# Windowed attention by key block, split low-rank products, and an earlier split of the third FFN tile

## What is computed

```python
def lora_proj(h, Wb, A, Bm, scale):
    return h @ Wb.T + h @ A.T @ Bm.T * scale
...
Q, K, V = (lora_proj(h, w, A, B, 1/16) for each of q, k, v)   # 16 heads of 128, rank 16
valid = (j <= i) & (j >= i - 63)                              # window of 64 keys
attn = softmax(rope(Q) @ rope(K).T / sqrt(128) + mask)
out  = lora_proj(attn @ V, wo, oA, oB, 1/16)
...
y = sum over experts e of cw[:, e] * (silu(x @ wg[e].T) * (x @ wu[e].T)) @ wd[e].T   # + a shared expert
```

## Time and profile before

| | |
|---|---|
| median of 3 runs | 1549.61 us (1549.12 to 1550.35) |
| the profiled execution | 1545.96 us, span 1544.1 us |
| PE busy | 1426.9 us, 92% of the span |
| VectorE (DVE), ScalarE (ACT), GpSimd (POOL) busy | 1112.4, 856.4, 627.5 us |
| first attention | up to about 338 us |
| output projection, first FFN, second attention | to 396, to about 630, to about 1265 us |
| second projection and second FFN | the rest |

### The profile page before, as it was taken

The page is one execution under the profiler, slowest core; times in us unless marked ns, Lnnn a source line. Parts: engine busy times, 40 slices in busy tenths (PEclk is TensorE's granted clock), DMA queues, the critical chain, the costliest instruction groups (busy, mean ns, idle before and its releaser), DMA issues.

```text
span 1544.1 us, 27763 instructions
## 1 busy us (share of the span) xinstructions
PE 1426.9 (92%) x8632; PEld 1197.3 (78%) x8632; DVE 1112.4 (72%) x2132; ACT 856.4 (55%) x1917; POOL 627.5 (41%) x540
## 2 busy tenths in 40 slices
PE   6999999999899999788988889789898989899998
PEld 4888888888788888667776777667777769688887
DVE  5666666657565556579999998899999977565555
ACT  1444444454343333477777777677777765433332
POOL 3555555530000001376868686668686620000000
PEclk8999999999999999999999999999999999999999
DMA  3000000001111112110101010101010001111110
GB/s 110 25 25 26 25 24 24 16 23 44 49 42 51 41 51 73 38 28 21 35 18 39 15 39 17 33 20 37 17 28 18 18 21 43 49 52 51 41 51 28
DMA packets 30138, 54.25 MB, mean 35 GB/s; under 512 B 6273, under 2 KB 13761, under 8 KB 29761
## 3 DMA queue, kind: packets, MB, share of 16 engines
q1 hardware_dynamic: 30016, 52.78, 11.7%
HBM read 39.13 MB, written 1.05 MB: 26 GB/s over the span
## 4 chain that ended last, share of the span: by engine, by line
PE 69%; DVE 14%; issue 9%; ACT 4%; POOL 1%; DVEq 0%; ACTq 0%; POOLq 0%
PE ps L1187 49%; PE ps L1388 8%; PE ps L1495 6%; PE ps L1333 5%; DVE pt_lo L706 3%; DVE nmb L691 2%; DVE qh L683 2%; PE ps L1275 2%; DVE qh L681 2%; ACT pt_hi L1106 1%; DVE rb L408 1%; ACT pb_low L1096 1%; DVE ot L714 1%; DVE h_lo L600 1%; DVE hf L594 1%
## 5 line engine op out<-in xcount | busy, mean ns | idle before, releaser
L706 DVE TENSOR_TENSOR pt_lo<-ps,pt_hi 128x512 fp32r<-128x512 f32 (+3 forms) x384 | 206.5, 549 | 36.3 <-ACT pt_hi L1106 34.0
L1187 PE MATMUL ps<-kh,qh 128*128 128x512 f32 (+3 forms) x768 | 194.5, 362 | 19.9 <-DVE qh L683 10.8
L1106 ACT CAST pt_hi<-ps 128x512 fp32r<-128x512 f32 (+3 forms) x384 | 176.0, 480 | 60.0 <-PE ps L1495 53.7
L691 DVE TENSOR_REDUCE nmb<-ps 128x1 f32<-128x1024 f32 (+7 forms) x256 | 191.0, 746 | 14.7 <-PE ps L1187 13.3
L1187 PEld LDWEIGHTS ps<-kh,qh 128*128 128x128 f32 x768 | 135.7, 192 | 48.8 <-ACT pb_low L1096 10.3
L1187 PE MATMUL ps<-xt_hi,wf_hi 128*128 128x512 f32 x400 | 160.7, 402 | 9.4 <-DVE wf_lo L522 9.4
L1187 PE MATMUL ps<-pt_hi,vst 128*128 128x512 f32 (+3 forms) x384 | 163.5, 426 | 0.0
L1187 PE MATMUL ps<-xt_hi,wf_lo 128*128 128x512 f32 x400 | 159.3, 398 | 0.0
L1187 PE MATMUL ps<-xt_lo,wf_hi 128*128 128x512 f32 x400 | 159.3, 398 | 0.0
L1032 ACT CAST h_hi<-hf 128x512 fp32r<-128x512 f32 x100 | 62.1, 621 | 137.8 <-DVE hf L594 137.8
L588 DVE TENSOR_TENSOR sg<-sg,cwu 128x512 f32<-128x512 f32 x88 | 62.2, 707 | 105.2 <-ACT sg L1026 105.1
(11 more groups left out here) (169 smaller groups left out, 4082.7 us busy)
## 6 DMA issues: line engine op xcount, KB each, us to landing
wf<-in_wf SPq DMA_DIRECT2D x50, 384.0 KB, 3.0
rb<-raw SPq DMA_DIRECT2D x192, 64.0 KB, 2.0
wa<-in_wa SPq DMA_DIRECT2D x16, 384.0 KB, 3.0
wb<-in_wb SPq DMA_DIRECT2D x8, 384.0 KB, 3.0
wo<-in_wo_a SPq DMA_DIRECT2D x16, 128.0 KB, 2.0
wo<-in_wo_b SPq DMA_DIRECT2D x16, 128.0 KB, 2.0
lb<-in_lb SPq DMA_DIRECT2D x16, 72.0 KB, 3.0
x_res<-in_x SPq DMA_DIRECT2D x4, 256.0 KB, 3.6
```

What stands on the lines that cost most here:

```text
L691: v.tensor_reduce(nmb[:, par, i:i + 1], ps[:, b:b + 2, :].rearrange("p b k -> p (b k)")[:, 0:P * (t + 1)], AX.X, ALU.max, negate=True).the ...
L706: v.tensor_tensor(pt_lo[:, s % 3, at], ps[:, 4 + s % 2, at], pt_hi[:, s % 3, at].bitcast(F32), ALU.subtract).then_inc(sem("b_pt_lo"), 1)
L1106: s_.copy(pt_hi[:, s % 3, at], ps[:, 4 + s % 2, at]).then_inc(sem("b_pt_hi"), 1)
L1187: return t_.matmul(o, l, r, start=start, stop=stop)
```

## The change

- **Values and products.** `xt_hi`, `xt_lo` lose their padding; values are made for eight tiles of 128 keys that are aligned with the query tiles, in four pieces. A key tile is seen by its own query tile and by the first 64 queries of the next, 192 queries, so `products` goes over key tiles: one fp32 matmul of 192 columns each, cut in two where it crosses a PSUM bank. `turn` transposes two squares of 128 and up to two blocks of 64 by 128, `pt` copies 320 or 384 columns instead of 512, and `pta` holds a whole head for each of two heads. The pieces of `products` hold one, two, two and three key tiles, and the third and fourth have new due times.
- **Low-rank products.** `la` and `lb` are loaded twice over (rows 0 to 47 and 64 to 111 of 128). ScalarE casts `lb` to `lb_hi` (`low_rank_hi`), VectorE makes `lb_lo` of 64 rows (`low_rank_lo`), and `lora` is four fp32r matmuls of one pass. `wef` has one buffer instead of two, so `weff(h)` waits for the split of head h-1. The output's `oa` (all heads, one load at the start) and `ob` are split ahead of head 14's steps, 80 rows each, and `low_rank_a` is one fp32r matmul.
- **Third FFN tile.** Its cast and its low part move into the end of the output projection, for both FFNs; the SP program is not changed there.

```diff
-            pta = sb("pta", [P, 2, HALF], c=own)
+            pta = sb("pta", [P, 2, NT * KW], c=own)
...
+            def low_rank_lo(h, u):
+
+                dve.wait_ge(sem("a_lb_hi"), h + 1)
+                v.tensor_tensor(lb_lo[0:LO, u, :], lb[0:LO, u, :], lb_hi[0:LO, u, :].bitcast(F32),
+                                ALU.subtract).then_inc(sem("a_lb_lo"), 1)
+
             def weff(h, u):
...
-                after(dve, "a_w_hi", h - 1)
-                after(dve, "a_w_lo", h - 1)
+                after(dve, "a_w_hi", h)
+                after(dve, "a_w_lo", h)
...
             def head_a(i, ip, u):
-                for kind, dh, n in steps_a(("weff", "rope", "max", "inv"), i, u):
+                if isinstance(i, int) and 2 * i + u == HA - 2:
+
+                    dve.wait_ge(sem("a_oa_hi"), 1)
+                    v.tensor_tensor(oa_s[LO:OR, :, :], oa[LO:OR, :, :], oa_s[LO:OR, :, :].bitcast(F32),
+                                    ALU.subtract).then_inc(sem("a_oa_lo"), 1)
+                    v.tensor_tensor(ob_s[32:LO, :], ob[32:LO, :], ob_s[32:LO, :].bitcast(F32),
+                                    ALU.subtract).then_inc(sem("a_oa_lo"), 1)
+                for kind, dh, n in steps_a(("lb_lo", "weff", "rope", "max", "inv"), i, u):
...
-                    elif h == 14:
+                    elif h == 13:
                         ffn_weight_lo(nxt, 1, 1, 1)
+                    elif h == 15:
+                        ffn_weight_lo(nxt, 2, 2, 0)
...
-                w_lo(2, 2, 0)
...
+            def low_rank_hi(h, u):
+                act.wait_ge(sem(f"lb_loaded{u}"), loads(h, u, 16))
+                after(act, "a_lora", h - 1)
+                s_.copy(lb_hi[:, u, :], lb[:, u, :]).then_inc(sem("a_lb_hi"), 1)
...
+                if isinstance(i, int) and 2 * i + u == HA - 2:
+
+                    act.wait_ge(sem("oa_loaded"), 16)
+                    act.wait_ge(sem("a_ob_loaded"), 16)
+                    act.wait_ge(sem("a_lora"), HA)
+                    s_.copy(ob_s[:, :], ob[:, :])
+                    s_.copy(oa_s[:, :, :], oa).then_inc(sem("a_oa_hi"), 1)
...
                     elif h == 12:
                         ffn_weight_hi(nxt, 1, 1, 1)
+                    elif h == 14:
+                        ffn_weight_hi(nxt, 2, 2, 0)
...
-                ffn_weight_hi(s, 2, 2, 0)
...
                 for c in range(NC):
-                    last = mm(ps[:, c, 0:3 * P], la[:, c, :], lb[:, u, :])
+                    mm(ps[:, c, 0:3 * P], las[:, c, :], lb_hi[:, u, :], True, False)
+                    last = mm(ps[:, c, 0:3 * P], las[0:LO, c, :], lb_lo[0:LO, u, :], False, True)
...
             def products_a(h, i, ip, u, n):
                 pe.wait_ge(sem("a_pt"), 4 * h + n + 1)
-                pe.wait_ge(sem("a_vout"), 5 * i + n + 2)
-                for m in range(2):
-                    t = 2 * n + m
-                    o = ps[:, 2 + 2 * u + t // 4, P * (t % 4):P * (t % 4) + P]
-                    for b in range(2):
-                        last = mm(o, va[:, ip, t + b, u, :], pta[:, n % 2, P * (2 * m + b):P * (2 * m + b) + P],
-                                  b == 0, b == 1)
+                pe.wait_ge(sem("a_vout"), 4 * i + n + 1)
+                for b in range(max(0, 2 * n - 1), 2 * n + 1 if n < 3 else NT):
+                    q, end = P * b, min(P * b + KW, T)
+                    while q < end:
+                        w = min(end, HALF * (q // HALF) + HALF) - q
+                        last = t_.matmul(ps[:, 2 + 2 * u + q // HALF, q % HALF:q % HALF + w], va[:, ip, b, u, :],
+                                         pta[:, u, KW * b + q - P * b:KW * b + q - P * b + w],
+                                         start=b == 0 or q == HALF > P * b, stop=True, skip_group_check=True)
+                        q += w
...
-    "products": [3717, 5961, 10934, 11408],
+    "products": [3717, 5961, 8000, 10934],
...
-    "o_out": [6909, 10401],
+    "o_out": [8300, 10401],
...
+    "lb_hi": [-29900],
+    "lb_lo": [-29800],
```

More of the change, by code:

```diff
@@ L27 @@
 PAD = WIN
[L28 to L29 removed]
 KW = WIN + P
 RANK = 16
+LR = 3 * RANK
+LO = 64
+OR = 80
 LORA_SCALE = 1.0 / RANK
@@ L121, in build @@
             wa = sb("wa", [P, 2, NC, 3, P], c=own)
-            lb = sb("lb", [3 * RANK, 2, 3 * P], c=own)
-            la = sb("la", [3 * RANK, NC, P], c=own)
-            wef = sb("wef", [P, 2, NC, 3, P], c=own)
+            lb = sb("lb", [P, 2, 3 * P], c=own)
+            lb_hi = sb("lb_hi", [P, 2, 3 * P], F32R, own)
+            lb_lo = sb("lb_lo", [P, 2, 3 * P], F32R, own)
+            la = sb("la", [P, NC, P], c=own)
+            las = sb("las", [P, NC, P], F32R, own)
+            wef = sb("wef", [P, NC, 3, P], c=own)
             wqk_hi = sb("wqk_hi", [P, 2, NC, 2, P], F32R, own)
@@ L922, in exps, with pt_out @@
                     t = 2 * n + m
-                    last = s_.activation(pa[:, t, 0:KW], ps[:, bank, KW * m:KW * m + KW], ACT.Exp,
+                    last = s_.activation(pa[:, t, WIN:2 * P], ps[:, bank, KW * m:KW * m + KW], ACT.Exp,
                                          bias=nmax[:, t:t + 1], accum_out=rsum[:, t:t + 1])
                 last.then_inc(sem("a_exp"), 1)
-            def pt_out(h, n):
+            def pt_out(h, u, n):
                 act.wait_ge(sem("a_turned"), 4 * h + n + 1)
-                after(act, "a_pv", 4 * h + n - 1)
-                s_.copy(pta[:, n % 2, :], ps[:, 6 + n % 2, :]).then_inc(sem("a_pt"), 1)
+                after(act, "a_pv", 4 * h - 4)
+                first, w = chunk_a(n)
+                s_.copy(pta[:, u, first:first + w], ps[:, 6 + n % 2, 0:w]).then_inc(sem("a_pt"), 1)
             def o_out(h, u, half):
-                act.wait_ge(sem("a_pv"), 4 * h + 2 * half + 2)
+                act.wait_ge(sem("a_pv"), 4 * h + half + 3)
                 s_.copy(ot[:, half, h, :],
@@ L957, in head_a @@
                         out_weight_hi("a", h)
-                for kind, dh, n in steps_a(("w_hi", "v_out", "exp", "pt", "o_out"), i, u):
+                if isinstance(i, int) and 2 * i + u == HA - 2:
[4 more added lines that the diff above has]
+                    s_.copy(oa_s[:, :, :], oa).then_inc(sem("a_oa_hi"), 1)
+                for kind, dh, n in steps_a(("lb_hi", "w_hi", "v_out", "exp", "pt", "o_out"), i, u):
                     h = 2 * i + u + dh
-                    if kind == "w_hi":
+                    if kind == "lb_hi":
+                        low_rank_hi(h, (u + dh) % 2)
+                    elif kind == "w_hi":
                         w_hi(h, i + (u + dh) // 2, (u + dh) % 2)
@@ L1245, in values @@
                 else:
-                    pe.wait_ge(sem("a_vout"), 5 * i + piece - 1)
-                for m in range(2 if piece < 4 else 1):
+                    pe.wait_ge(sem("a_vout"), 4 * i + piece - 1)
+                for m in range(2):
                     t = 2 * piece + m
                     last = three(ps[:, piece % 2, 2 * P * m:2 * P * m + 2 * P],
-                                 lambda c, a: xt(a, c, P * t - PAD, P),
+                                 lambda c, a: xt(a, c, P * t, P),
                                  lambda c, b: (wv_hi, wv_lo)[b][:, c, :, :].rearrange("p u d -> p (u d)"))
@@ L1273, in turn_a @@
                 after(pe, "a_pt", 4 * h + n - 1)
-                for m in range(4):
-                    last = t_.transpose(ps[:, 6 + n % 2, P * m:P * m + P],
-                                        pa[:, 2 * n + m // 2, P * (m % 2):P * (m % 2) + P], idf[:, :])
-                last.then_inc(sem("a_turned"), 1)
+                at = WIN if n else 0
+                t_.transpose(ps[:, 6 + n % 2, at:at + P], pa[:, 2 * n, P:2 * P], idf[:, :])
+                if n:
+                    t_.transpose(ps[:, 6 + n % 2, 0:WIN], pa[0:WIN, 2 * n, 0:P], idf[0:WIN, 0:WIN])
@@ L1638, in steps_a, with chunk_a @@
     return [step[1:] for step in sorted(found)]
+def chunk_a(n):
+    first = max(0, 2 * n * KW - WIN)
+    return first, 2 * n * KW + KW + P - first
 def head_at(g, gp, hh, dh):
```

108 lines of the change are left out of this document (61 added, 47 removed).

## The result

The changed kernel took 1555.93 us in the median of 6 runs (1554.15 to 1562.22), against 1550.11 (1549.12 to 1551.85) before: ratio 1.0041, 95% interval 1.0023 to 1.006. It is 0.4% slower, where 1.4% faster was forecast.

What follows compares the result with a forecast made beforehand. PE was taken to bound the first attention and the output projection. Steady heads -16.8, attention start -2 and end +2.7, projection -7.7 and third tile +2 gave -21.8 us, a median of 1528 (range 1505 to 1542).

Steps and rivals of the forecast that it cites:

- Transposes: Turns in each attention head: fewer whole squares, 64-column ones at 0.045 to 0.09 us; 0.25 us less a head.
- Low-rank product: Each attention head: four fp32r matmuls of 384 columns at 0.18 us instead of 1.55 us; 0.8 us less.
- Products: Products in each attention head: 18 passes instead of 32; 0.78 us less a head (0.77 to 0.87).
- Values: Value matmuls in the attention: six of 256 columns fewer for two heads, 0.7 us less.
- Output projection: First half of the first output projection: period per head 1.7 us instead of 2.26; 7.7 us less (5 to 9).
- Who is late next: Inside heads: PE waits before `scores(h, 3)` and the third `turn`; 0.8 to 1.4 us a head, 2.0 taken for two.
- Start and end of the attention: First heads 2 us less (0 to 4); last heads, with the `oa` split at head 14, 2.7 more (0 to 5).
- Third tile: Start of both FFNs: later residual and `z` replace the `wf_lo` wait; +2 us in sum (0 to +6).
- The clock: Rival, 6%: granted clock falls at waits ahead of `turn`, once a head, 24 us eating the gain (1552), possibly slower.
- `lb_lo` meets GpSimd: Rival, 12%: the `lb_lo` subtraction lasts 1 us longer beside GpSimd in 14 heads, +14 us, 1542.

Runs made afterwards that it cites:

- e4: Changed kernel with the low-rank matmuls and the turns' transposes all over 128 rows: 1545.01 us, ratio 0.9972 to the kernel before.
- e6: e4 with the cast of `lb` moved ahead of a head's last exp and its subtraction behind the fourth maximum: 1547.64 us, ratio 0.9994.
- e10: e5 with the third FFN tile's split back in its old place and the split of `lb` one head earlier: 1529.77 us, ratio 0.9867.
- e11: e4 without the low-rank part in the heads: product in fp32 over 48 rows, no split of `lb`: 1543.44 us, ratio 0.9958.
- e5: e4 with the split of `oa` in four pieces, three of them moved into the output projection: 1538.36 us, ratio 0.9932.
- e7: e6 with `oa` split in four pieces as in e5 and the output projection's low-rank matmul over 128 rows: 1543.02 us, ratio 0.9957.
- e12: Kernel before the change with only the move of the third FFN tile's split, in both FFNs: 1548.34 us, ratio 0.9993.

## Why the prediction was wrong

It had -21.8 us; it was +5.8 in the medians.

- **Transposes** and **Low-rank product** are the steps that failed. Forecast were 0.5 and 1.6 us less for two heads; measured were 1.78 more and none (4.87 for 3.09, 2.99 for 2.97). I took issue distances of runs of equal matmuls for an order in which the row count goes back and forth between 128 and 64. Without the switches (e4 against the changed kernel, the waits of 0.9 us taken off) turns cost 3.2 and low-rank matmuls 1.6 us (e6): the switches cost some 3 us for two heads. The Trainium skill (TensorE: Matmul & The Clock Gate, "Step-by-step: what each phase is for") says that the row count doesn't matter for a load's time. The trace agrees for its length (186 and 183 ns), not for its start. TensorEngine Tiling (Array Packing), "Key Properties", of the Trainium skill says that a change of tiling mode drains TensorE; the loads that start with their own matmuls between 128 and 64 rows fit this, and I hadn't weighed it; no run reads the mode itself. The trace of before held a hint that I passed over: 0.21 us from a product to the 48-row matmul, where products are 0.11 apart.
- The 64-column transposes: put at 0.045 to 0.09, they take 0.11, as whole ones do. (0.09 was a misreading too: it divides 0.36 us by four, but the three distances inside are 0.11, and only other work follows after 0.03.) Even without switches they save nothing.
- **Products** -1.56, measured -1.70: close by luck, since 0.69 us of the measured 5.57 are waits ahead of the third turn, without which it is -2.39. **Values** -0.7, measured -0.67: right. **Output projection** -7.7, measured -7.6: right.
- **Who is late next**: right in place and size once TensorE's work did fall. 2.0 us for two heads forecast; in e4 1.6 ahead of scores(h, 3) and the third turn and 0.65 for `kr`, the rotation that the forecast names. The share of `lb_lo` is small: moved away (e10) or left out (e11), it leaves 0.3 of the third turn's 0.36 us, which come from TensorE's being early. In the changed kernel the switches hid half of the first two waits. Without switches two heads gained 1.6 (e4) against 2.4 forecast; the 2.5 of e10 comes with one wait fewer than the forecast had.
- **Start and end of the attention**: the end had the right cause and was too small, +6.4 for +2.7; e5 takes it to +1.1. The start was wrong in sign: +10.2 in the profiled run up to head 8, where -2 and the first pairs' -2.4 each were forecast. 2.8 us of it are there before the first `qk` piece (26.0 for 23.2). Then TensorE waits for `pa` four times, 6.0 us in all (at 73.9, 97.3, 117.8 and 142.7 us), once in each of the four heads in which VectorE also has to make `z` and `x_res`:

```profile
97.33 0.33 PE L1316 MATMUL ps<-idf,pa 128*128 128x128 f32 x1 [1.50 <-POOL pa L819]
...
117.80 0.33 PE L1316 MATMUL ps<-idf,pa 128*128 128x128 f32 x1 [1.49 <-POOL pa L819]
```

The kernel before has no wait over 0.8 us there; e10 still has the four (5.9 us). The forecast took its slacks from a steady head and had no term for this. 10.2 us at half clock lie in it as well (from 98.3 and 118.7 us), which cost up to 5.1.

- **Third tile**: +2 forecast, of it +1 for `up` of tile 2 in each FFN (measured +1.7 in the first); the residual came at 410.19, 5.9 us behind the last projection matmul, and waits for `z` and `h_lo` replaced that for `wf_lo`, as described. The size is between -1 and +3.
- **The clock** was the rival on the slower side, and part of it came: the clock fell, three times, not in each head, 17 us at half in all. For the last heads the runs tie it to the waits for `oa`. The two in the first heads begin 1.0 and 0.9 us behind the waits at 97.3 and 117.8, but e4 has four such waits of 1.59 us and no fall there, so what decides stays open. The rival `lb_lo` meets GpSimd came where I moved it (1.27 us for 0.56), and in the changed kernel once in 16 heads (1.30).

## What to carry to other kernels

Price a matmul by the distance in its own order: a change between 128 rows and 64 costs 0.04 to 0.19 us each time, and zero rows that keep the count at 128 are cheaper; a change between 128 and 80 cost nothing here. A small new operation costs by what stands behind it in its queue: the same 0.5 us cast and subtraction were worth 7 us when moved one head earlier, and one large split in four pieces took 4.2 us off the last heads and put 2.0 on the projection. When the bounding engine's work falls, check the two or three smallest slacks first, and in the heads in which another engine has extra work too.

## What the runs showed of the hardware

- A switch between 128 and 64 rows: 0.37 us for 0.18 between fp32r matmuls of 384 columns, whose loads take 0.19; 0.20 (to 64) and 0.15 (to 128) for 0.11 between transposes, whose loads take 0.14. A switch from 128 to 80 rows: 0.12 us, as without one (e5, e7).
- A transpose of 64 x 128 behind another one is spaced like one of 128 x 128, 0.11 us.
- A VectorE subtraction of 128 x 384 with both inputs in SBUF takes 0.55 us alone and 1.27 to 1.31 beside a GpSimd addition (e6, e10).
- All 23 stretches at half clock in the heads of the fourteen profiled kernels, 3.4 or 6.8 us each, begin within or up to 1.9 us behind a wait of TensorE of 1.1 to 1.9 us; most such waits have none behind them. Before and e12 have neither.
- The second attention took 609.2 to 617.6 us with no edit there and had 34 to 63 us at half clock; the two go together only loosely (e7: 612.3 with 61.6, e12: 616.1 with 54.8).
